# Output projection as twelve F32R products of two-part operands in a fused attention and expert layer

## What is computed

```
xn = layernorm(x)
q, k, v = xn @ Wq, xn @ Wk, xn @ Wv        # 16 heads of 64
scores = q @ k.T + bias                    # 512 x 512 for each sequence and head
ctx = softmax(scores) @ v                  # 512 x 1024 for each sequence
x = x + ctx @ Wo                           # Wo is 1024 x 128: the output projection
x = x + experts(layernorm(x))              # top 4 of 16, 128 -> 512 -> 128, gelu
```

## Time and profile before

| | |
|---|---|
| median of 3 runs | 1105.16 us (1104.22 to 1105.43) |
| the profiled execution's own time | 1105.33 us |
| its span in the trace | 1103.4 us |
| granted TensorE clock over the span | 0.985 of full |
| TensorE busy (matmuls) | 1048.9 us, 95% |
| TensorE busy (weight loads) | 851.4 us, 77% |
| VectorE, ScalarE, GpSimd busy | 76%, 75%, 62% |

### The profile page before, as it was taken

The page is one execution under the profiler, slowest core; times in us unless marked ns, Lnnn a source line. Parts: engine busy times, 40 slices in busy tenths (PEclk is TensorE's granted clock), DMA queues, the critical chain, the costliest instruction groups (busy, mean ns, idle before and its releaser), DMA issues.

```text
span 1103.4 us, 26950 instructions
## 1 busy us (share of the span) xinstructions
PE 1048.9 (95%) x8345; PEld 851.4 (77%) x8346; DVE 839.2 (76%) x2610; ACT 829.6 (75%) x2040; POOL 682.4 (62%) x900
## 2 busy tenths in 40 slices
PE   8999999999999999999999999999897889999992
PEld 4777777777777777777777777777797878999991
DVE  6888888889888888888888888887474544456684
ACT  5888888788888888788788888877674546766660
POOL 3654456765775676577577657747666665566552
PEclk9999999999999999999999999999999899999996
DMA  7576666775776676677577666778423322222554
GB/s 214 160 213 187 194 170 174 215 207 164 213 204 181 176 227 193 168 221 204 159 202 222 184 176 199 236 241 253 154 80 113 97 66 71 65 70 80 181 153 153
DMA packets 135192, 188.61 MB, mean 171 GB/s; under 512 B 18599, under 2 KB 108464, under 8 KB 135056
## 3 DMA queue, kind: packets, MB, share of 16 engines
q1 hardware_dynamic: 126352, 170.01, 54.0%
q0 software_dynamic: 8704, 16.93, 4.5%
HBM read 100.52 MB, written 87.39 MB: 170 GB/s over the span
## 4 chain that ended last, share of the span: by engine, by line
PE 84%; DVE 5%; issue 3%; another core or an unknown queue 2%; DMA 2%; ACT 1%; SPq 1%; POOL 1%; DVEq 0%; POOLq 0%; ACTq 0%
PE bank L1567 16%; PE bank L1581 10%; PE bank L1749 10%; PE bank L1620 10%; PE bank L1636 10%; PE bank L1647 5%; PE bank L1518 4%; PE bank L1520 4%; PE bank L1519 4%; PE bank L1735 2%; PE bank L1733 2%; PE bank L1734 2%; PE bank L1705 1%; DVE yb L1414 1%
## 5 line engine op out<-in xcount | busy, mean ns | idle before, releaser
L984 POOL TENSOR_SCALAR shared<-shared,rinv 128x512 f32<-128x512 f32 x512 | 351.8, 699 | 243.5 <-DVE rinv L1249 240.9
L1058 ACT ACTIVATE shared<-shared,nmax 128x512 f32<-128x512 f32 x512 | 368.5, 733 | 73.0 <-DVE nmax L1243 52.9
L1243 DVE CUSTOM_DVE_ANT_0 shared<-bank,shared 128x512 f32<-128x512 f32 x512 | 330.1, 682 | 85.9 <-issue 35.0
L1025 POOL DMA_INDIRECT y_dram<-yb,home x144 | 155.4, 1079 | 111.4 <-issue 90.2
L1749 PE MATMUL bank<-shared,act_h 128*128 x1152 | 147.3, 282 | 19.1 <-DVE yb L1414 15.1
L1265 DVE STREAM_TRANSPOSE turned<-shared 128x512 f32<-128x512 f32 x248 | 160.9, 687 | 0.0
L1064 ACT ACTIVATE pt_e<-bank 128x512 f32<-128x512 f32 x256 | 144.9, 594 | 19.0 <-PE bank L1581 18.6
L399 POOL DMA_INDIRECT xs_dram<-copies,slot x128 | 134.2, 1049 | 39.1 <-issue 28.1
L1749 PEld LDWEIGHTS bank<-shared,act_h 128*128 128x128 f32 x1152 | 138.1, 196 | 24.6 <-issue 24.3
L1581 PE MATMUL bank<-idn,shared 128*128 128x128 f32 x1024 | 136.8, 276 | 0.5 <-DVE nmax L1243 0.5
L1581 PEld LDWEIGHTS bank<-idn,shared 128*128 128x128 f32 x1024 | 112.8, 141 | 24.0 <-issue 14.5
(11 more groups left out here) (229 smaller groups left out, 1876.9 us busy)
## 6 DMA issues: line engine op xcount, KB each, us to landing
pt_dram<-turned SPq DMA_DIRECT2D x496, 128.0 KB
pt_d<-pt_dram SPq DMA_DIRECT2D x124, 512.0 KB
xb<-xs_dram SPq DMA_DIRECT2D x64, 130.0 KB
shared<-in_experts SPq DMA_DIRECT2D x16, 514.0 KB
yk_sb<-y_dram SPq DMA_DIRECT2D x32, 256.0 KB
shared<-roll_dram SPq DMA_DIRECT2D x4, 768.0 KB, 8.4
y_dram<-yb,home POOLq DMA_INDIRECT x144
xs_dram<-pad_sb SPq DMA_DIRECT2D x17, 130.0 KB
```

The lines of the kernel that those rows point to most:

```text
L984: pool.tensor_scalar(tile, tile, rinv[:, 2 * v + hh:2 * v + hh + 1], 1.0, ALU.mult, ALU.mult)\
L1025: pool.indirect_dma_start(y_dram, bass.IndirectOffsetOnAxis(ap=home[:, j, c:c + 1], axis=0), yb[:, j, c, :], None, bounds_check=last_row, ...
L1058: act.activation(prob[:, v, hh, :], prob[:, v, hh, :], ACT.Exp, bias=nmax[:, n:n + 1], scale=-1.0, accum_out=rsum[:, n:n + 1]).then_inc(ex ...
L1243: dve.tensor_tensor_reduce(prob[:, v, hh, :], score_bank(v, hh)[:], strips[:, 2 * i + hh, v * P:v * P + S], -1.0, BIG, ALU.add, ALU.min, n ...
```

## The change

The context gets two parts: ScalarE writes `ctxt_hi` in F32R where it wrote `ctxt`, and VectorE writes `ctxt_lo` as the difference, as the first instruction of its step. Wo gets two parts once, in step (0, 1): it is loaded into the unused head of `shared`, rounded by ScalarE and subtracted by VectorE. `project_out` makes three F32R products for each of the four chunks of 128 tokens, twelve of 128 stationary and 128 moving columns. The semaphore `ctxt_rdy`, which VectorE raises, takes the place of `c_cp` in `project_out` and in the scores of chunk 3. The space for the descriptors of GpSimd's DMAs is set to 8192 bytes.

```diff
+        wo_stage = shared[:, 0:NPR * D].rearrange("p (n d) -> p n d", n=NPR)
...
-        wo_sb = sb("wo_sb", [P, NPR, D], stack=attn)
+        wo_hi = sb("wo_hi", [P, NPR, D], F32R, attn)
+        wo_lo = sb("wo_lo", [P, NPR, D], F32R, attn)
...
-        ctxt = sb("ctxt", [P, S], stack=attn)
+        ctxt_hi = sb("ctxt_hi", [P, S], F32R, attn)
+        ctxt_lo = sb("ctxt_lo", [P, S], F32R, attn)
...
-            sp.dma_start(wo_sb[:], wo.rearrange("(n p) d -> p n d", p=P)).then_inc(ld_wo, 16)
+            sp.dma_start(wo_stage, wo.rearrange("(n p) d -> p n d", p=P)).then_inc(ld_wo, 16)
...
-                act.activation(ctxt[:, ::-1], ps_a[:], ACT.Copy).then_inc(c_cp, 1)
+                act.activation(ctxt_hi[:, ::-1], ps_a[:], ACT.Copy).then_inc(c_cp, 1)
...
+                if (b, i) == (0, 1):
+                    act.wait_ge(ld_wo, 16)
+                    act.activation(wo_hi[:], wo_stage, ACT.Copy).then_inc(wo_hi_rdy, 1)
...
+            def context_lo(b, i):
+
+                dve.wait_ge(c_cp, b * NPR + i + 1)
+                dve.nop(nofuse=True)
+                dve.tensor_tensor(ctxt_lo[:, ::-1], ps_a[:], ctxt_hi[:, ::-1].bitcast(F32), ALU.subtract).then_inc(ctxt_rdy, 1)
...
                 if (b, i) == (0, 1):
+                    dve.wait_ge(wo_hi_rdy, 1)
+                    dve.tensor_tensor(wo_lo[:], wo_stage, wo_hi[:].bitcast(F32), ALU.subtract).then_inc(wo_rdy, 1)
                     routing_constants(0)
...
             def step(b, i):
-                up = pair_after(b, i, 1)
+                two, up = before(b, i, 2), pair_after(b, i, 1)
+                if exists(two[0]):
+                    context_lo(*two)
                 scores(b, i, 0, 0)
...
             def drain():
                 turned_lo(0, 0)
                 expert_lo(0, 0)
+                context_lo(LAST, NPR - 2)
                 turned_lo(1, 1)
                 expert_lo(1, 1)
                 turned_lo(2, 2)
                 expert_lo(2, 2)
                 finish(0, 0)
+                context_lo(LAST, NPR - 1)
...
                     if n >= 2:
-                        pe.wait_ge(c_cp, n - 1)
+                        pe.wait_ge(ctxt_rdy, n - 1)
...
             def project_out(b, i):
-                pe.wait_ge(c_cp, b * NPR + i + 1)
+                pe.wait_ge(ctxt_rdy, b * NPR + i + 1)
                 if i == 0 and exists(b - 1):
                     pe.wait_ge(res_rdy, b)
                 for c in range(TC):
-                    mm = pe.matmul(ps_o[:, c * D:(c + 1) * D], ctxt[:, c * P:(c + 1) * P], wo_sb[:, i, :],
-                                   start=(i == 0 and c == 0), stop=(i == NPR - 1), skip_group_check=True)
+                    tok = slice(c * P, (c + 1) * P)
+                    terms = ((ctxt_lo, wo_hi), (ctxt_hi, wo_lo), (ctxt_hi, wo_hi))
+                    for m, (ctxt, w) in enumerate(terms):
+                        mm = pe.matmul(ps_o[:, c * D:(c + 1) * D], ctxt[:, tok], w[:, i, :], start=(i == 0 and c == 0 and m == 0),
+                                       stop=(i == NPR - 1 and m == 2), skip_group_check=True)
...
-                    pe.wait_ge(ld_wo, 16)
+                    pe.wait_ge(wo_rdy, 1)
...
-    nc = bacc.Bacc("TRN2", target_bir_lowering=False, num_devices=1)
+    nc = bacc.Bacc("TRN2", target_bir_lowering=False, num_devices=1, dynamic_dma_scratch_size=8192)
```

More of the change, by code:

```diff
@@ L157, in layer_kernel @@
         params = shared[:, 0:NE * EW]
+        wo_stage = shared[:, 0:NPR * D].rearrange("p (n d) -> p n d", n=NPR)
+        assert NPR * D <= AHEAD
         attn = ctx.enter_context(ExitStack())
@@ L216, in layer_kernel @@
         c_rdy, c_cp, o_rdy, res_rdy = (sem(n) for n in ("c_rdy", "c_cp", "o_rdy", "res_rdy"))
+        ctxt_rdy, wo_hi_rdy, wo_rdy = sem("ctxt_rdy"), sem("wo_hi_rdy"), sem("wo_rdy")
         k2_rdy, kk_rdy, rk_rdy, lc_rdy = sem("k2_rdy"), sem("kk_rdy"), sem("rk_rdy"), sem("lc_rdy")
```

## The result

The changed kernel takes **1133.64 us** (median of 5 runs, 1131.52 to 1139.94), the kernel before, beside it, 1105.16 (5 runs, 1103.81 to 1106.88). The ratio is 1.0273, 95% interval 1.0250 to 1.0297: 28.5 us slower. The forecast of 1136.5 us was within 0.3%. How that sum came about is another question, to which the experiments turn.

What follows compares the result with a forecast made beforehand. In attention, the time was taken to be the sum of the distances between TensorE's instructions. Added to 1105.33 us, 27.7 + 1.8 + 1.0 + 0.8 = 31.3 gave 1136.6, forecast as 1136.5 us; range about 1125 to about 1157.

Steps and rivals of the forecast that it cites:

- The price of one product: Projection: twelve F32R products follow each other at the weight loads' pace, 0.112 us each, bounds 0.100 and 0.12.
- The products' sum: Projection: 0.454 us more in each of 61 calls that count, 27.7 us in all, bounds 18.9 and 33.6.
- what is added there is paid in full: Attention: time added to TensorE's chain lengthens the run fully, except in the few microseconds where the chain leaves TensorE.
- VectorE's subtraction: Start of VectorE's step: delays the first score tile by 0.26 us, costing 0.03 us a step, 1.8 us in all.
- both are tied: VectorE's delayed first and third score-tile reads end about when chunk 3's scores and its turning's second half start.
- Splitting Wo once: One-time rounding by ScalarE and subtraction by VectorE: 1.0 us, bounds 0 and 2.5.
- 743 to 781 us: Stretch with the chain off TensorE: three projection calls cost nothing, the subtraction in VectorE's part costs 0.8 us.
- TensorE waiting for VectorE: Rival: the 0.26 us delay is paid in each step, 15.3 us instead of 1.8, 1150 us; chance 0.10.
- F32R products of 128 columns: Rival for the projection: narrow ones need as many passes as fp32, 108 us more, 1217 us; chance 0.10.
- The shared load is dropped: Rival for the projection: two products share one load of ctxt_hi, leaving 8 loads, 1109 us; chance 0.02.
- Loads overlap more: Rival for the projection: loads come a quarter faster, 0.083 us a product, 1115.5 us; chance 0.03.
- faster: Rival for the projection: F32R loads go at the bf16 pace, twelve products take 0.70 us, 1097.5 us; chance 0.04.

Runs made afterwards that it cites:

- e3: Changed kernel with 64 instead of 128 moving columns in each of the twelve projection products: 1096.19 us, 25.6 more than before.
- e4: Changed kernel with 64 instead of 128 stationary columns in each of the twelve projection products: 1082.04 us, 11.4 more than before.
- e2: Changed kernel without VectorE's subtraction, the high part standing in for the low; twelve products and Wo split kept: 1089.15 us, ratio 1.0175.
- e11: Changed kernel with Wo stationary, three products of 512 moving columns, result turned back once a sequence, no subtraction or low part: 1076.47 us, ratio 1.0047.
- e1: Kernel before plus only the subtraction (result unused), its waits and the 8192 bytes of descriptor space: 1078.47 us, ratio 1.0082.
- e0: Kernel before with only the descriptor space of GpSimd's DMAs cut to 8192 bytes: 1106.54 us, ratio 1.0017.
- e7: The changed kernel itself run again on another chip, against the kernel before: 1131.25 us against 1104.28, ratio 1.0249.
- e6: Changed kernel with Wo stationary, three products of 512 moving columns, result turned back once a sequence, subtraction after VectorE's third score tile: 1120.30 us, ratio 1.0138.
- e10: Kernel before plus the subtraction over 384 of 512 columns (result unused), its waits and descriptor space: 1072.45 us against 1071.82.

## Why the prediction was right, and where it was not

The direction, the size and the mechanism held: twelve weight loads at their own pace on a path that is nearly all TensorE. Two terms of the sum were off in opposite directions, one by 9 us too much and one by 6 too little. That they nearly cancel is luck, and the total is better than its parts.

- **The price of one product.** Right. 0.112 us forecast, 0.108 on the average of a piece of twelve. e3 and e4 show that the load sets it, as the two rows of loads before matmuls of few columns said. The low end of my bounds, 0.100, was not reached. That the fp32 product "hides this limit" no run shows: its records follow each other at 0.111 us, which is the loads' own pace.
- **The products' sum: 27.7 us forecast, 18.5 measured** (e2; 16.0 to 21.5 by its interval; in the attention's steps 1 to 60 alone, 721.1 - 705.3 = 15.9). Some 0.6 us of it are the split of Wo, which e2 still makes. The median is just under my lower bound of 18.9, and the steps are clearly under it. The step that failed is "what is added there is paid in full". A piece of 1.29 instead of 1.34 takes 3 us off (61 x 0.05). The rest was swallowed: the plain step of before already waited 0.04 us for VectorE's sixth tile (the first piece of its value projection is 0.16 us, in the row shown with e11, and 0.12 in e2 and in the changed kernel), and in steps 3, 4 and 6, which have other work of TensorE with waits behind the projection, 0.18 or 0.19 of the 0.40 disappears (in step 3 the routing's turning, L346, goes from 0.55 to 0.44 and `weigh_late` from 1.93 to 1.88). Step 7, at 11.95 on average before and 12.06 in e2, swallows 0.28. A chain that goes from one TensorE instruction to the next says that TensorE was never idle for long; it does not say that a second path of equal length does not run beside it.
- **VectorE's subtraction: 1.8 us forecast, 7.9 measured** (e1; 5.8 to 11.8). That "both are tied" was right, by two errors that cancel. VectorE starts the subtraction 0.10 us after the copy's end and not 0.01, so its first tile is 0.33 us late and not 0.26; and its read reaches TensorE's load after 0.05 us, where I took 0.15 from a matmul. The failed step is the one after: I measured the slack to the matmul of chunk 3's scores, and it had to be measured to the weight load, which before stands at 302.20 and needs 0.10 us before its matmul. A release that comes for the matmul comes too late for the load, and costs the bare load, 0.10 us, in each step, instead of 0.03. The second part is step 5, for which I had put all delay into the upper bound: 0.40 us there by e1.
- **Splitting Wo once: 1.0 forecast.** Step 2, the only one that waits for it, is 12.87 us where a plain one is 12.01: 0.86.
- **743 to 781 us: 0.8 forecast.** Steps 60 to 62, from 731 to 768 us before, take 36.8 us where they took 37.0; nothing to be seen. The rest of the stretch is in the part behind step 63, which scatters by more than the term.
- **Descriptor space: 0.** Right within what ten runs can tell (e0).
- **The two calls in the drain**: 0.9 forecast. The part behind step 63 is 2.9 us longer in e7, on another chip, and 9.5 in the first profile. It scatters by more than the term.
- **Rivals.** TensorE waiting for VectorE was partly true, at a price of 0.10 and not 0.26 a step. F32R products of 128 columns are not slow (e2, e3). *The shared load is dropped* fell with the 768 loads of the trace (three groups of 256). *Loads overlap more* fell as well: the products follow each other at 0.108 us and not at 0.083. The Trainium skill's 81 ns for a pair of load and matmul of 128 columns ("TensorE: Matmul & The Clock Gate", section "Back-to-back issue gap") is not reached by the products here, whose operands have 4 bytes. And *faster* was mispriced as a rival: with a piece of 0.70 us, which I had priced at 1097.5 us, e11 shows plain steps unchanged at 11.51. In plain steps a faster projection brought nothing.

None of the kernels tried is faster than the one before. If the two-part projection is wanted, e6 is the cheapest of the four that compute all of it: 1.4% instead of 2.5% in the same set. Whether the plain step would be shorter if the value projection did not wait for the sixth tile was not tried.

## What to carry to other kernels

When a change trades passes for weight loads, count the loads: here 128 columns moving past 128 stationary ones of 4 bytes were bound by the load (1.26 us for twelve with half the moving columns), and fewer passes save nothing; make the operand stationary that lets the moving one be 512 wide. A release in the middle of a row of products has to be early enough for the next weight load to be made before its matmul's time, here by 0.10 us, and not only for the matmul. And before a gain or a cost is multiplied by the number of steps, look in the timeline for a wait on another engine that ends within some 0.05 us of TensorE's own work: beside such a tie a saving of 0.19 us a step was worth nothing here, and a cost of 0.40 was worth less than its length.

## What the runs showed of the hardware that was not expected

- A wait in TensorE's queue holds back the weight load behind it as well as the matmul. A load that normally stands 0.23 us ahead then stands right before its matmul and costs 0.10 us (e1); standing 0.16 ahead it costs 0.01 to 0.02 (e10).
- With the granted clock at 0.54 the products' pace is half: twelve products in 2.66 us, 0.21 each from 826.2 us on, where they take 1.29 at full speed.
- Products with 64 stationary and 128 moving columns follow each other at 0.73 / 12 = 0.061 us, where 128 stationary columns have 0.108.
- A subtraction with both inputs in SBUF takes VectorE 0.69 to 1.25 us, depending on what GpSimd does, and slows GpSimd's pair of multiplications from 1.37 to 1.80; one instruction waits while the other runs. With one input in PSUM it takes 0.66 to 0.70 throughout.
